# Cross-attention over 32 batches: context rows loaded as 120 and 5 partitions, a slot earlier, with all statistics of a batch in one VectorE slot

## The chip, the cores and the metric

One Trainium2 chip, one core. The metric is the device time of one execution in microseconds (us); the kernel before has three runs, and one profiled execution from which every row below is taken.

## The reference

Inputs are x (32 batches x 112 tokens x 512), a context (32 x 375 x 512), a mask (32 x 375, all true), four 512 x 512 weights, gamma, beta and a gate. All is float32.

```
a   = layer_norm(context) * gamma + beta          # over the 512 features of each of the 375 rows
Q   = x @ Wq.T ;  K = a @ Wk.T ;  V = a @ Wv.T     # split into 16 heads of 32
p   = softmax(mask(Q @ K.T / sqrt(32)))            # 112 x 375 for each batch and head
out = x + tanh(gate) * ((p @ V) @ Wo.T)
```

## The kernel before

**Layout.** The context comes in twice: transposed (`ctxT`, features on partitions) into `cn`, which is what K and V are computed from, and by rows (`ctx`) into `rows`, which serves the layer norm's statistics alone. `rows` holds one batch as 125 partitions of 3 context rows each (3 x 512 floats, 6 KB on a partition, 750 KB in all); there is one such buffer. VectorE computes `bn_stats` on the three chunks and `bn_aggr` on the results, GpSimd makes -mean and 1/std of them (`row_statistics`), SyncE stores these in DRAM (`row_stats`), and a broadcast load brings them back to all 128 partitions (`stat_bc`, 375 KB). GpSimd then centres, scales and applies gamma and beta to `cn`.

**Products.** K, V, Q and the output projection are each computed as three float32r products (high and low parts). A batch is four slots, u = 0 to 3, of four heads each; the loop body is LOOP = 8 slots, two batches. In slot r TensorE does the K projection of item r + 1, a V projection of one 125-row chunk (in slots u = 3, 0, 1) or the output projection (u = 2), the scores of item r and the weighted sum of item r - 3.

**The exchange of maxima.** The softmax maximum of each slot is found by going through DRAM. In slot r VectorE reduces the scores of item r - 1 (`quadrant_maxima`, L708), SyncE stores the result (L318, `row_max`, 21 KB) and, when that has landed, loads it back spread out (L323, `x4`, which the profile names x, 84 KB). VectorE in slot r + 1 reduces the loaded tile (L695), spreads it (L698) and subtracts it from the scores (L718); ScalarE exponentiates (L584). SyncE's part is strictly serial:

```python
sync.wait_ge(quad_max, i * LOOP + r)
if behind(i, LOOP, r - 1):
    wait_apart(sync, ld_max, i * (16 * LOOP) + (r - 1) * 16)
sync.dma_start(row_max.rearrange("t (q k) -> q t k", q=HC), rmax[:, :]).then_inc(max_stored, 16)
wait_apart(sync, max_stored, i * (16 * LOOP) + r * 16)
...
sync.dma_start(x4[:, :], bass.AP(...)).then_inc(ld_max, 16)
```

So there is one store and one load a slot, and the next store waits for the last load. The order within each engine's slot is written by hand:

- VectorE: `quadrant_maxima` of item r - 1, `row_maximum` and `subtract_maximum` of item r - 2, at u = 3 `normalise`, at u = 0 the low part of the attention output, at u = 1 the statistics' first chunk, at u = 2 the other two chunks and `bn_join`, and then at u = 2 `result` (L689), which empties the PSUM bank of the output projection. TensorE's V projection in the slot after (u = 3) waits for that (`y_done`), because it writes the same bank.
- ScalarE: `scores_out` of item r - 1 (L553), the exponentials of item r - 3 (L584), `weighted_out` (L569); at u = 3 the three loads on its own DMA queue, in the order statistics (L259), transposed context (L247), rows (L253); then the copy of K out of PSUM (L606), the high part of the context (L521) and the copy of V (L613).
- The rows load of batch c + 5 waits for `stats_done` of batch c + 4, as there is one `rows` buffer. `stats_done` is what `bn_join` signals.

Ahead of the slots is a prologue: weights and x come in, Q is computed for all batches, and the rows of batches 0 to 3 are loaded from SyncE's queue (L253 as well) and their statistics computed.

Of the kernel before, what the change touches and what calls it, by code (L numbers as in the profile page):

```python
# [12 lines left out]
B, T, S, D = 32, 112, 375, 512  # L13
# [3 lines left out]
ST, SP_ = 3, 125  # L17
# [16 lines left out]
def xattn(nc, xT, x, ctx, ctxT, mask, wqT, wkT, wvT, woT, gamma, beta, gate, out, row_stats):  # L34
    es = ExitStack()
    with es:
        def sb(name, shape, dt=F32):
            return es.enter_context(nc.sbuf_tensor(name, shape, dt))

        def sem(name):  # L40
            return es.enter_context(nc.semaphore(name))
# [64 lines left out]
        rows = sb("rows", [128, ST, D])  # L106
# [32 lines left out]
        ld_rows = sem("ld_rows")  # L139
# [27 lines left out]
        stats_done = sem("stats_done")  # L167
        ln_step = sem("ln_step")
        row_stat_done = sem("row_stat_done")
# [35 lines left out]
        rows_v = ctx.rearrange("b (p j) d -> b p j d", j=ST)  # L205
# [5 lines left out]
        def live(i, k, shift, count):  # L211
            return not isinstance(i, int) or 0 <= k * i + shift < count

        def behind(i, k, shift):
            return not isinstance(i, int) or k * i + shift > 0

        def first_two(i, c):
            return isinstance(i, int) and 2 * i + c < 2

        def wait_apart(engine, s, value):  # L220
            engine.wait_ge(s, value)
            if not isinstance(value, int):
                engine.sem_inc(passed)
# [19 lines left out]
        def is_slot(i, r, n):  # L243
            return isinstance(i, int) and LOOP * i + r == n

        def load_ctx(queue, i, c):
            queue.dma_start(cn[:, c % 2, :, :], ctxT_v[i * 2 + c, :, :, :]) \  # L247
                .then_inc(ld_ctx[c % 2], 16)

        def load_rows(queue, i, c):  # L250
            if behind(i, 2, c):
                wait_apart(queue, stats_done, i * 2 + c)
            queue.dma_start(rows[0:SP_, :, :], rows_v[i * 2 + c, :, :, :]).then_inc(ld_rows, 16)  # L253

        def load_stats(queue, i, c):
            wait_apart(queue, stat_stored, i * 32 + (c + 1) * 16)
            if behind(i, 2, c):
                wait_apart(queue, divided, i * LOOP + c * KT)
            queue.dma_start(stat_bc[:, :, :].rearrange("p w s -> p (w s)"),  # L259
                           row_stats[bass.ds(i * 2 + c, 1), :].partition_broadcast(128)  # L260
                           .rearrange("p a s -> p (a s)")).then_inc(ld_stat, 16)
# [229 lines left out]
        def _(act):  # L491
# [52 lines left out]
            def scores_out(i, r):  # L544

                c, u = divmod(r - 1, KT)
                act.wait_ge(s_mm, i * LOOP + r)
                if u == 0:
                    act.wait_ge(bias_done, i * 2 + (c + 1))
                if isinstance(i, int) and LOOP * i + r - 1 < NB:  # L550
                    act.wait_ge(low_done, r)
                for j in range(ST):
                    act.activation(prob[0:SP_, (r - 1) % NB, j, :].rearrange("p (h t) -> p h t", h=HC),  # L553
                                   sbank[0:SP_, :, T * j:T * j + T], ACT.Identity,
                                   bias=mask_b[0:SP_, c % 2, j:j + 1]).then_inc(s_out, 1)
# [16 lines left out]
            def slot(i, r):  # L572
                c, u = divmod(r, KT)
                if is_slot(i, r, 0):
                    act.wait_ge(mask_mm, 1)
                    act.activation(maskT[0:SP_, :, :],
                                   bank[PB][0:SP_, 0:ST * B].rearrange("p (j b) -> p j b", j=ST),
                                   ACT.Copy).then_inc(mask_out, 1)
                if live(i, LOOP, r - 1, SLOTS):
                    scores_out(i, r)  # L580
                if live(i, LOOP, r - 3, SLOTS):
                    for j in range(ST):
                        act.wait_ge(sub_done, i * (LOOP * ST) + ((r - 3) * ST + j + 1))
                        act.activation(prob[0:SP_, (r - 3) % NB, j, :], prob[0:SP_, (r - 3) % NB, j, :],  # L584
                                       ACT.Exp, scale=SCALE).then_inc(exp_done, 1)
                if live(i, LOOP, r - 4, SLOTS):
                    weighted_out(i, r)
                if u == 3:
                    if live(i, 2, c + 3, B) and behind(i, 2, c + 1):
                        load_stats(act, i, c + 3)  # L590
                    if live(i, 2, c + 3, B) and not first_two(i, c + 3):
                        wait_apart(act, c_done, i * LOOP + (c + 2) * KT)
                        load_ctx(act, i, c + 3)
                    if live(i, 2, c + 5, B) and behind(i, 2, c + 2):
                        load_rows(act, i, c + 5)
                if u == 0 and live(i, 2, c - 2, B):
                    b = c - 2
                    act.wait_ge(o_norm, i * 2 + (b + 1))
                    if behind(i, 2, b):
                        act.wait_ge(y_mm, i * 2 + b)  # L600
                    act.activation(oT[:, 0, :, :].rearrange("p c t -> p (c t)"),
                                   pv[:, b % 2 * HT:b % 2 * HT + HT], ACT.Copy).then_inc(o_hi, 1)

                if live(i, LOOP, r + 1, SLOTS):
                    act.wait_ge(k_mm, i * LOOP + (r + 2))
                    act.activation(kT[:, (r + 1) % 2, :], bank[KB][:, 0:SE], ACT.Copy) \  # L606
                        .then_inc(k_done, 1)
                if not early(i, r):
                    context_hi(i, r)
                vc, j = v_item(r)  # L610
                if j is not None and live(i, 2, vc, B):
                    act.wait_ge(v_mm, i * (2 * ST) + (vc * ST + j + 1))
                    act.activation(v_sb[0:SP_, vc % 2, j, :], bank[VO[r % 2]][0:SP_, :], ACT.Copy) \  # L613
                        .then_inc(v_done, 1)

            slots(act, slot)

        @block.vector
        def _(dve):
# [20 lines left out]
                split(xraw[:, g, :, :], xr[:, g, 0, :, :], xr[:, g, 1, :, :],  # L640
                      xr_hi, i * 2 + g, xr_done)

            def bn_rows(i, c, chunks):
                if chunks[0] == 0:
                    dve.wait_ge(ld_rows, i * 32 + (c + 1) * 16)
                    if not first_two(i, c):
                        dve.wait_ge(row_stat_done, i * 2 + (c - 1))
                    if isinstance(i, int) and 2 * i + c > 0:
                        dve.wait_ge(stats_done, 2 * i + c)
                for j in chunks:  # L650
                    dve.bn_stats(stats[0:SP_, j, :], rows[0:SP_, j, :]).then_inc(bn_step, 1)  # L651

            def bn_join(i, c):
                wait_apart(dve, bn_step, i * (2 * ST) + (c + 1) * ST)
                for j in range(ST):
                    last = dve.bn_aggr(mv[0:SP_, c % 2, j, :], stats[0:SP_, j, :])  # L656
                last.then_inc(stats_done, 1)

            def statistics(i, c):
                bn_rows(i, c, range(ST))  # L660
                bn_join(i, c)

            def weight_lo(n, raw, dst):
                for k in range(KT):
# [70 lines left out]
            def slot(i, r):  # L735
                c, u = divmod(r, KT)
                if live(i, LOOP, r - 1, SLOTS):
                    quadrant_maxima(i, r)
                if live(i, LOOP, r - 2, SLOTS):
                    row_maximum(i, r)  # L740
                    subtract_maximum(i, r)
                if u == 3 and live(i, 2, c - 1, B):
                    normalise(i, c - 1)
                if u == 0 and live(i, 2, c - 2, B):
                    b = c - 2
                    dve.wait_ge(o_hi, i * 2 + (b + 1))
                    dve.tensor_tensor(oT[:, 1, :, :].rearrange("p c t -> p (c t)"),  # L747
                                      pv[:, b % 2 * HT:b % 2 * HT + HT],
                                      oT[:, 0, :, :].rearrange("p c t -> p (c t)").bitcast(F32),
                                      ALU.subtract).then_inc(o_done, 1)  # L750
                if u == 1 and live(i, 2, c + 4, B) and behind(i, 2, c + 2):
                    bn_rows(i, c + 4, (0,))
                if u == 2 and live(i, 2, c + 4, B) and behind(i, 2, c + 2):
                    bn_rows(i, c + 4, (1, 2))
                    bn_join(i, c + 4)
                if u == 2 and live(i, 2, c - 2, B):
                    result(i, c - 2)

# [187 lines left out]
```

## Time and profile before

| | |
|---|---|
| runs (us) | 1159.52, 1155.87, 1161.36; median 1159.52 |
| profiled execution's own time | 1151.25 us |
| span in the profile | 1149.4 us |
| mean granted TensorE clock | 0.953 |
| busy | PE 89%, PEld 74%, DVE 67%, POOL 59%, ACT 56% |
| DMA | 102.26 MB, 89 GB/s mean; ScalarE's queue (q10) 56.60 MB, SyncE's (q1) 44.94 MB |

PE is TensorE, PEld its weight loads, DVE VectorE, ACT ScalarE, POOL GpSimd, SP SyncE; SPq and ACTq are the issuing queues of those engines. In a wait row the engine and its line stand left of the arrow, and what it waited for right of it. A clock of 1.00 is 2.4 GHz, 0.50 is 1.2 GHz. Most runs agree closely, and a difference of under 0.5% can't be told from none.

### The profile page before, as it was taken

What the parts mean: (1) busy time and instruction counts of PE and PEld (TensorE: products, weight loads), DVE (VectorE), ACT (ScalarE), POOL (GpSimd) and SP (SyncE); (2) the same over time, 40 slices, a digit from 0 to 9 for tenths busy, and PEclk for the clock granted to TensorE, in tenths of its full rate; (3) what the DMA queues carried; (4) which work ended last, traced back from release to release, by engine and by line L of the source; (5) the groups of instructions that cost most, each with busy time, mean ns of one, the idle gap of its engine ahead of it and who ended that gap; (6) DMA issues with size and microseconds to landing.
All of it is one profiled execution on the core that took longest, in us unless ns stands there. A gap on an engine that the chain in (4) does not pass through costs nothing.

```text
span 1149.4 us, 31949 instructions
## 1 busy us (share of the span) xinstructions
PE 1025.9 (89%) x11665; PEld 852.0 (74%) x11665; DVE 774.2 (67%) x1446; ACT 645.2 (56%) x1332; POOL 680.7 (59%) x945
## 2 busy tenths in 40 slices
PE   8796989989989989899898889898889898999995
PEld 7795877778777767687777767777777677878873
DVE  4640477776676677667666777666767866787775
ACT  2312565665565656565556656655556566666662
POOL 1346866666666756567557556676566556776211
PEclk9898999999999999999999999999999999999997
DMA  9443222222232332223323322232233222322111
GB/s 274 158 148 71 98 78 75 88 72 86 86 97 87 97 95 82 66 75 89 95 86 97 94 80 78 66 96 87 87 96 95 84 78 68 94 76 73 33 33 40
DMA packets 82772, 102.26 MB, mean 89 GB/s; under 512 B 28544, under 2 KB 65408, under 8 KB 82720
## 3 DMA queue, kind: packets, MB, share of 16 engines
q10 hardware_dynamic: 24232, 56.60, 15.1%
q1 hardware_dynamic: 58488, 44.94, 14.5%
q8 instruction: 35, 0.57, 0.2%
q14 instruction: 17, 0.14, 0.0%
HBM read 91.34 MB, written 10.19 MB: 88 GB/s over the span
## 4 chain that ended last, share of the span: by engine, by line
DMA 65%; DVE 16%; PE 12%; issue 4%; POOL 2%; SPq 1%; ACT 0%; DVEq 0%; ACTq 0%; POOLq 0%
DMA row_max<-rmax 34%; DMA x<-row_max 25%; PE bank L765 9%; DVE rmax L708 4%; DVE shared_f L718 3%; DVE stats L651 3%; DMA rows<-in_ctx 3%; DMA row_stats<-row_stat 3%; DVE bank L698 2%; PE sbank L859 1%; DVE top L695 1%; PE bank L875 1%; DVE mv L656 1%; DMA shared_f<-in_xT 1%; POOL cn L408 0%
## 5 line engine op out<-in xcount | busy, mean ns | idle before, releaser
L765 PE MATMUL bank<-w_v,shared_r 128*125 128x512 f32 x1152 | 312.5, 424 | 77.0 <-DVE xy L689 77.0
L765 PEld LDWEIGHTS bank<-w_v,shared_r 128*125 128x125 f32 x1152 | 229.6, 202 | 135.9 <-issue 84.2
L708 DVE TRANSPOSE_TENSOR_REDUCE rmax<-shared_f 128x14 f32<-128x448 f32 x384 | 216.3, 614 | 158.5 <-DMA row_max<-rmax 131.1
L765 PE MATMUL bank<-shared_r,w_k 128*128 128x376 f32 x1536 | 300.7, 345 | 10.1 <-ACT shared_f L606 9.5
L765 PEld LDWEIGHTS bank<-shared_r,w_k 128*128 128x128 f32 x1536 | 260.8, 190 | 32.2 <-issue 20.9
L584 ACT ACTIVATE shared_f<-shared_f 125x448 f32<-125x448 f32 x384 | 204.3, 580 | 133.9 <-DVE shared_f L718 133.8
L438 POOL TENSOR_TENSOR shared_f<-shared_f 125x448 f32<-125x448 f32 x128 | 151.0, 1179 | 177.9 <-ACT shared_f L584 164.7
L553 ACT ACTIVATE shared_f<-sbank,mask_b 125x448 f32<-125x448 f32 x384 | 215.6, 635 | 69.2 <-PE sbank L859 69.1
L718 DVE TENSOR_TENSOR shared_f<-shared_f,bank 125x448 f32<-125x448 f32 x384 | 215.5, 617 | 4.5
L613 ACT ACTIVATE shared_f<-bank 125x512 f32<-125x512 f32 x96 | 57.3, 597 | 160.2 <-PE bank L765 160.1
L695 DVE TENSOR_REDUCE top<-x 128x14 f32<-128x168 f32 x128 | 56.0, 437 | 120.9 <-DMA x<-row_max 120.9
L859 PEld LDWEIGHTS sbank<-shared_f 32*125 32x125 f32 x3072 | 96.3, 185 | 49.6 <-issue 49.2
L428 POOL TENSOR_TENSOR shared_r<-cn,shared_r 128x375 fp32r<-128x375 f32 x128 | 117.7, 920 | 21.5 <-ACT shared_r L521 20.4
L408 POOL TENSOR_TENSOR cn<-cn,stat_bc 128x375 f32<-128x375 f32 x128 | 116.4, 943 | 20.6 <-DMA stat_bc<-row_stats 16.8
L392 POOL TENSOR_SCALAR row_stat<-mv 125x3 f32<-125x3 f32 x32 | 8.0, 251 | 202.4 <-DVE mv L656 202.4
L859 PE MATMUL sbank<-shared_f 32*125 32x112 f32 x3072 | 119.0, 284 | 0.8 <-ACT shared_f L553 0.8
L414 POOL TENSOR_TENSOR cn<-cn,stat_bc 128x375 f32<-128x375 f32 x128 | 118.7, 962 | 0.2
L875 PE MATMUL bank<-shared_f 125*32 125x112 f32 x3072 | 101.2, 265 | 12.5 <-ACT shared_f L569 12.3
L765 PE MATMUL bank<-w_o,shared_r 128*112 128x512 f32 x384 | 97.1, 402 | 4.0 <-DVE shared_r L747 4.0
L606 ACT ACTIVATE shared_f<-bank 128x376 f32<-128x376 f32 x128 | 61.9, 483 | 56.3 <-DVE mv L656 49.8
L875 PEld LDWEIGHTS bank<-shared_f 125*32 125x32 f32 x3072 | 70.0, 110 | 27.9 <-ACT shared_f L569 15.3
L698 DVE STREAM_TRANSPOSE bank<-top 128x448 f32<-128x448 f32 x128 | 84.5, 660 | 4.4
(64 smaller groups left out, 950.6 us busy)
## 6 DMA issues: line engine op xcount, KB each, us to landing
cn<-in_ctxT ACTq DMA_DIRECT2D x30, 750.0 KB, 6.2
rows<-in_ctx ACTq DMA_DIRECT2D x28, 750.0 KB
stat_bc<-row_stats ACTq DMA_DIRECT2D x29, 375.0 KB, 4.2
x<-row_max SPq DMA_DIRECT2D x128, 84.0 KB
xy<-in_x SPq DMA_DIRECT2D x32, 224.0 KB, 3.1
out<-xy SPq DMA_DIRECT2D x32, 224.0 KB, 4.9
shared_f<-in_xT SPq DMA_DIRECT2D x7, 896.0 KB, 8.4
rows<-in_ctx SPq DMA_DIRECT2D x4, 750.0 KB
```

What stands on the lines that cost most here:

```text
L408: pool.tensor_tensor(cn[:, c % 2, k, :], cn[:, c % 2, k, :], stat_bc[:, 0, :], ALU.add).then_inc(centred, 1)
L414: pool.tensor_tensor(cn[:, c % 2, k, :], cn[:, c % 2, k, :], stat_bc[:, 1, :], ALU.mult).then_inc(divided, 1)
L428: pool.tensor_tensor(cT[:, p, 1, k, 0:S], cn[:, p, k, :], cT[:, p, 0, k, 0:S].bitcast(F32), ALU.subtract) \
L438: pool.tensor_tensor(psum[0:SP_, :], prob[0:SP_, q, 0, :], prob[0:SP_, q, 1, :], ALU.add).then_inc(sum_done, 1)
L553: act.activation(prob[0:SP_, (r - 1) % NB, j, :].rearrange("p (h t) -> p h t", h=HC), sbank[0:SP_, :, T * j:T * j + T], ACT.Identity, bias ...
L584: act.activation(prob[0:SP_, (r - 3) % NB, j, :], prob[0:SP_, (r - 3) % NB, j, :], ACT.Exp, scale=SCALE).then_inc(exp_done, 1)
L698: dve.transpose(spread.rearrange("p (k a) -> p k a", a=32), top[:, :].unsqueeze(2).to_broadcast([128, BLK, 32])) \
L708: last = dve.tensor_reduce(rmax[:, BLK * j:BLK * j + BLK], prob[:, (r - 1) % NB, j, :].rearrange("p (k a) -> p k a", a=32), AX.X, ALU.max, ...
L718: dve.tensor_tensor(prob[0:SP_, (r - 2) % NB, j, :], prob[0:SP_, (r - 2) % NB, j, :], spread[0:SP_, :], ALU.subtract).then_inc(sub_done, 1)
L765: last = pe.matmul(dst, l, m, start=(start and k == 0), stop=(stop and k == len(pairs) - 1))
L859: last = pe.matmul(bank[h][0:SP_, T * j:T * j + T], kT[part, r % 2, SP_ * j:SP_ * j + SP_], qs[part, c % 2, u, :], start=True, stop=True)
L875: pe.matmul(bank[PB][HD * h:HD * h + HD, 0:T], v_sb[0:SP_, c % 2, j, col:col + HD], prob[0:SP_, (r - 3) % NB, j, T * h:T * h + T], start=( ...
```

## The change

`load_rows` issues two transfers in place of one: partitions 0 to 119 and partitions 120 to 124, both on the same semaphore, so that a batch now counts 32 in place of 16. On ScalarE the rows load moves from slot u = 3, where it stood behind the statistics and context loads, to slot u = 2, directly after `weighted_out`. On VectorE `bn_rows` and `bn_join` become one function; all three `bn_stats` and the three `bn_aggr` now run in slot u = 1, and slot u = 2 has no statistics any more. The bytes moved and the arithmetic are the same. `load_rows` serves the prologue's four loads too.

```
@@ load_rows @@
             if behind(i, 2, c):
                 wait_apart(queue, stats_done, i * 2 + c)
-            queue.dma_start(rows[0:SP_, :, :], rows_v[i * 2 + c, :, :, :]).then_inc(ld_rows, 16)
+            for part in (slice(0, 120), slice(120, SP_)):
+                queue.dma_start(rows[part, :, :], rows_v[i * 2 + c, part, :, :]).then_inc(ld_rows, 16)
@@ ScalarE, slot @@
                         load_ctx(act, i, c + 3)
-                    if live(i, 2, c + 5, B) and behind(i, 2, c + 2):
-                        load_rows(act, i, c + 5)
+                if u == 2 and live(i, 2, c + 5, B) and behind(i, 2, c + 2):
+                    load_rows(act, i, c + 5)
@@ VectorE @@
-            def bn_rows(i, c, chunks):
-                if chunks[0] == 0:
-                    dve.wait_ge(ld_rows, i * 32 + (c + 1) * 16)
...
-            def bn_join(i, c):
+            def statistics(i, c):
+                dve.wait_ge(ld_rows, i * 64 + (c + 1) * 32)
+                if not first_two(i, c):
+                    dve.wait_ge(row_stat_done, i * 2 + (c - 1))
+                if isinstance(i, int) and 2 * i + c > 0:
+                    dve.wait_ge(stats_done, 2 * i + c)
+                for j in range(ST):
                     dve.bn_stats(stats[0:SP_, j, :], rows[0:SP_, j, :]).then_inc(bn_step, 1)
                 wait_apart(dve, bn_step, i * (2 * ST) + (c + 1) * ST)
                 for j in range(ST):
                     last = dve.bn_aggr(mv[0:SP_, c % 2, j, :], stats[0:SP_, j, :])
                 last.then_inc(stats_done, 1)
...
@@ VectorE, slot @@
                 if u == 1 and live(i, 2, c + 4, B) and behind(i, 2, c + 2):
-                    bn_rows(i, c + 4, (0,))
-                if u == 2 and live(i, 2, c + 4, B) and behind(i, 2, c + 2):
-                    bn_rows(i, c + 4, (1, 2))
-                    bn_join(i, c + 4)
+                    statistics(i, c + 4)
```

## Rows read from the trace of the kernel before

**Rows 1.** The page: busy time of the engines, chain that ended last.

```profile
PE 1025.9 (89%) x11665; PEld 852.0 (74%) x11665; DVE 774.2 (67%) x1446; ACT 645.2 (56%) x1332; POOL 680.7 (59%) x945
...
DMA 65%; DVE 16%; PE 12%; issue 4%; POOL 2%; SPq 1%; ACT 0%; DVEq 0%; ACTq 0%; POOLq 0%
```

**Rows 2.** Waits in 259.6 to 946.5 us: total, times, longest (us).

```profile
DVE rmax L708 <- DMA row_max<-rmax: 102.2, 21, 5.4
...
PE bank L765 <- DVE xy L689: 65.9, 21, 4.3
```

**Rows 3.** Stretches: length; PE, PEld, DVE, ACT, POOL busy; clock; DMA share; GB/s.

```profile
259.60:946.50 686.90, 618.19 (x7397) 507.97 (x7396) 482.42 (x925) 406.08 (x840) 435.04 (x610) 0.96 0.29 86
...
1041.00:1111.00 70.00, 70.00 (x891) 58.54 (x884) 52.05 (x93) 46.35 (x99) 28.47 (x32) 1.00 0.14 38
```

**Rows 4.** Timeline of SyncE's queue: start, duration, instruction.

```profile
514.58 0.54 SPq L318 DMA_DIRECT2D row_max<-rmax  x1
516.87 0.54 SPq L323 DMA_DIRECT2D x<-row_max  x1
521.47 0.53 SPq L318 DMA_DIRECT2D row_max<-rmax  x1
531.11 0.53 SPq L323 DMA_DIRECT2D x<-row_max  x1
534.50 0.53 SPq L318 DMA_DIRECT2D row_max<-rmax  x1
...
540.59 0.56 SPq L318 DMA_DIRECT2D row_max<-rmax  x1
...
547.47 0.54 SPq L318 DMA_DIRECT2D row_max<-rmax  x1
```

**Rows 5.** Timeline of ScalarE and its queue, slots u = 2 and 3.

```profile
511.63 0.47 ACT L606 ACTIVATE shared_f<-bank 128x376 f32<-128x376 f32 x1
...
518.44 0.39 ACTq L247 DMA_DIRECT2D cn<-in_ctxT  x1
519.27 0.29 ACTq L253 DMA_DIRECT2D rows<-in_ctx  x1
```

**Rows 6.** Timeline of TensorE: K projection, then V projection, of slot u = 3.

```profile
515.19 2.32 PE L765 MATMUL bank<-shared_r,w_k 128*128 128x376 f32 x12
519.91 4.59 PE L765 MATMUL bank<-w_v,shared_r 128*125 128x512 f32 x12 [2.39 <-DVE xy L689]
```

**Rows 7.** Timeline of VectorE: statistics at the end of slots u = 1 and 2.

```profile
510.79 0.69 DVE L651 BATCH_NORM_STATS2 stats<-rows 125x6 f32<-125x512 f32 x1
...
517.30 1.28 DVE L651 BATCH_NORM_STATS2 stats<-rows 125x6 f32<-125x512 f32 x2
...
519.01 0.75 DVE L689 SCALAR_TENSOR_TENSOR xy<-bank,gat,xy 112x512 f32<-112x512 f32 x1
```

**Rows 8.** Busy time by stretch, columns as in rows 3.

```profile
525.00:527.00 2.00, 2.00 (x59) 1.72 (x53) 1.25 (x2) 1.71 (x5) 2.00 (x4) 1.00 0.33 137
...
1010.00:1012.00 2.00, 2.00 (x27) 1.45 (x29) 1.93 (x4) 0.51 (x1) 1.67 (x4) 1.00 0.90 324
```

**Rows 9.** ScalarE's queue at the last context load, which no rows load follows.

```profile
1034.90 0.45 ACTq L247 DMA_DIRECT2D cn<-in_ctxT  x1
```

**Rows 10.** SyncE's queue: first u = 3 store, the last two, and the load after.

```profile
135.66 0.53 SPq L318 DMA_DIRECT2D row_max<-rmax  x1
...
1009.92 0.53 SPq L318 DMA_DIRECT2D row_max<-rmax  x1
...
1035.83 0.53 SPq L318 DMA_DIRECT2D row_max<-rmax  x1
1041.09 0.53 SPq L323 DMA_DIRECT2D x<-row_max  x1
```

**Rows 11.** Waits in 95 to 120 us, where the slots begin.

```profile
PE bank L765 <- ACT shared_f L606: 9.5, 1, 9.5
```

**Rows 12.** The page: packets, MB and share of ScalarE's DMA queue.

```profile
q10 hardware_dynamic: 24232, 56.60, 15.1%
```

More of the change, by code:

```diff
@@ L641, in x_group @@
                       xr_hi, i * 2 + g, xr_done)
-            def bn_rows(i, c, chunks):
-                if chunks[0] == 0:
-                    dve.wait_ge(ld_rows, i * 32 + (c + 1) * 16)
[L646 to L650, printed above, removed]
+            def statistics(i, c):
[5 more added lines that the diff above has]
+                for j in range(ST):
                     dve.bn_stats(stats[0:SP_, j, :], rows[0:SP_, j, :]).then_inc(bn_step, 1)
-            def bn_join(i, c):
                 wait_apart(dve, bn_step, i * (2 * ST) + (c + 1) * ST)
@@ L657, in bn_join @@
                 last.then_inc(stats_done, 1)
-            def statistics(i, c):
-                bn_rows(i, c, range(ST))
-                bn_join(i, c)
             def weight_lo(n, raw, dst):
```

## The prediction

> **What bounds the kernel now.** I read four views in this order. The page first: TensorE is busy 89% of the span, yet the chain that ended last is 65% DMA and 12% PE [rows 1]. So there are two candidates for the bound, and they must be held against each other in the steady part. The waits of the loop say how they meet: TensorE's only large wait is the V projection on VectorE's `result` (`y_done`), 65.9 us in 21 batches, 3.1 each, and VectorE's largest is on the store of the maxima, 102.2 us, 4.9 each [rows 2]. The stretches give both lengths. The store of slot u = 3 comes first at 135.66 and last with a rows load at 1009.92, 27 batches later: 874.3 / 27 = 32.38 us a batch [rows 10]. From 1041 to 1111, where no rows or context load is left, TensorE is busy all 70 of 70 us at clock 1.00 and does ten slots, 28.0 us a batch [rows 3]. So TensorE's floor is 28.0, and 4.4 us a batch are someone else's.
>
> SyncE's queue shows whose. Name by L0, L1 the landing of the exchange's load in slots u = 0 and 1; the next store is issued there. The four intervals between stores of one batch are 6.9 (u = 2 to 3), 13.0 (u = 3 to 0), 6.1 and 6.9 [rows 4]. The 13.0 is a store that takes 9.64 where its neighbour takes 2.29, and a load of 3.39. The context load was issued 3.0 us ahead of it, and the rows load 2.2 ahead [rows 4, 5]. The store ends at 531.1, 11.8 us after the rows load was issued, and the rows load is what it waits out: from 525 to 527 the DMA engines are busy 0.33 of 16, about five engines, moving 137 GB/s, while a context load of the same 750 KB, with nothing behind it, keeps them at 0.90 and 324 GB/s [rows 8]. At the last context load, which no rows load follows, the store waits only until 6.2 us after the context's issue [rows 9, 10]. TensorE then pays twice: it waits 2.39 for `result`, and its V projection takes 4.59 us [rows 6]; mean clock in the loop is 0.96 against 1.00 later [rows 3].
>
> **The change part by part.**
>
> *The split.* Before, the load runs on about 5 of 16 engines for its whole length. The new 120-partition piece has no row before. From below: 750 KB at the 324 GB/s of rows 8 is 2.4 us, plus the 2.3 that a bare store takes from issue to landing [rows 4], 4.7. From above: the 6.2 of the context load, which had the 375 KB of statistics ahead of it. The two-issue form adds one 0.29 us issue [rows 5]. I take 5.2 + 0.3 = 5.5, nearest to the like-sized context load less the statistics' share (375 KB / 324 = 1.2). Range 4.7 to 6.5. On ScalarE 28 more issues of 0.29 are 8 us, on an engine that is 56% busy: nothing on the path, unless it is what TensorE waits for.
>
> The Trainium skill ("DMA: Bandwidth & Descriptors", section on why a DMA increments its semaphore by 16) says that a transfer uses the largest number up to 16 that divides the slowest dimension: 5 for 125 partitions, 15 for 120, 5 for 5, and 4 for the exchange, whose DRAM side leads with 4. The trace agrees: ScalarE's queue has 24232 packets [rows 12], and its 30 context loads at 512 + 16 and its 33 statistics and x loads at 128 + 16 leave 3640, which is 28 x (125 + 5). By this rule the busiest engine carries 54 KB in place of 150, at 137 / 5 = 27 GB/s some 2.0 us, and the load lands 4.3 us after its issue, just under my lower bound; the sum below would not change, since the context load then ends last.
>
> *The statistics on VectorE.* Slot u = 2 loses the stretch from 517.30 to 519.01, 1.7 us [rows 7], ahead of `result`: `y_done` comes 1.7 us sooner after the subtraction. Slot u = 1 gains it: 0.7 becomes 2.4. There, after L0: reduce, spread and subtract end at 517.30 - 514.58 = 2.7, statistics 2.4, maxima of the next slot 1.7 (from 519.76 to the store at 521.47): L0 + 6.8. The interval from L0 to L1 is 6.9, so the store at L1 is not late, by 0.1; if the u = 0 interval's store got faster, it would be late by up to 1. I book 0.1.
>
> *The moved rows load.* ScalarE now waits in slot u = 2 for `stats_done` at L0 + 5.1. Before, it started the K copy at 511.63 [rows 5], 0.8 us after the statistics began; now the two issues are done 2.4 + 0.6 = 3.0 after that begin, so the K copy, the high part and the next slot's `scores_out` stand 2.2 us later. Cover: the next K projection starts at 515.19 [rows 6], 3.1 us after the K copy's end before: 0.9 is left. If this cover were gone it would cost up to 2.2 a batch. At u = 3 ScalarE loses its wait on the statistics.
> The DMA side: issued at L0 + 5.4 = L1 - 1.5, landed at L1 + 4.0. The store of slot u = 2, issued at L1 + 0.1, would land at L1 + 2.4 and now lands with it: 1.6 late. Load 3.4: the slot u = 3 store is issued at L1 + 7.5. The context load goes out 1.1 us after the subtraction (518.44 against 517.30), L1 + 3.9, and lands 6.2 later, L1 + 10.1; the store would have landed at L1 + 9.8, so 0.3 late; with its load the exchange is at L1 + 13.5. Adding 6.1 and 6.9: 26.5 us. If rows and context load delay each other in full (6.5 for rows, context later by the 2.4 of its data), it is 28.9. GpSimd's `row_statistics` no longer waits, since its input is there a slot earlier.
>
> *Sum.* The exchange needs 26.5 to 28.9, TensorE 28.0. With two loops of nearly one length the slower sets the pace and neither gets its slack back at once: I take 28.3. 27 x (32.38 - 28.3) = 110 us. The batches behind 1009.92 have no rows load and stay.
> *Prologue.* The slots' start waits 9.5 us [rows 11] for a ScalarE that stands behind the statistics of batch 3, whose rows were under way beside a context load. Landing some 6 us sooner, as in 11.8 against 5.5, gives 6 (3 to 9.5).
> Against its own time: 1151.25 - 110 - 6 = 1035. The runs' median is 8.3 above that time; part of it should be the disturbed exchange itself, so I carry half: 1039.
>
> **The rivals.**
> 1. *The split does not spread the load.* The move alone then works. Rows at 137 GB/s take 750 / 137 = 5.5, plus 2.3: 7.8 from issue, landing L1 + 6.3; the store of u = 2 is 3.9 late, the next is issued at L1 + 9.8, context is landed by then or soon after, and two slots take 15.5: 28.5 to 29.5 a batch, 27 x 3.4 + 3 = 95 saved, 1060. For it: nothing in the trace shows a 120-partition load. Against it: the 0.33 beside the 0.90 [rows 8]. The Trainium skill (same page, "Rules for kernel authors") says not to bother with two transfers on disjoint partition halves, as they share the engines and serialise; for this load of 125 partitions, whose one form fills a third of the engines, rows 8 speak against applying it.
> 2. *DMA still ends last.* The u = 3 store meets the context load at its worst, as at 1035.83 where it took 5.26 [rows 10], 3.0 over a bare one, the u = 2 store is 2.4 late, and the K copy's 2.2 comes through half: 5.8 + 2.4 + 5.7 + 3.0 + 13.0 + 1.1 = 31.0; saved 27 x 1.4 + 6 = 44, 1111. For it: exchange is 65% DMA now. Against: the two delays come one after the other, and cover each other.
> 3. *Slower: two collisions in place of one.* Rows and context loads met the exchange in one slot before; now each meets its own store. If the rows load at u = 2 costs the 7.35 it costs at u = 3, and the context load its 3.0, a batch is 24.5 + 10.4 = 34.9, 27 x 2.5 = 68 more, on the median 1227. It decides once the two delays together pass 32.4 - 24.5 = 7.9. Against it: my terms are 1.6 and 0.3, and in rival 1 3.9.
>
> **How the numbers follow.** Forecast 0.68, own range 1026 (28.0 a batch and 9.5 in the prologue give 1024, with nothing of the 8.3) to 1055. Rival 1 0.15, rival 2 0.11, rival 3 0.04, and 0.02 for no difference. With 0.2 left outside: 1024 to 1085, which holds the forecast and most of rival 1. A measurement here tells no change from 0.5%. Faster 0.94, same 0.02, slower 0.04.
>
> **What would show it.** In the trace after: the u = 3 store under 4 us, the u = 2 store 3 to 5; u = 3 stores 28 to 29 us apart; no stretch at 0.33 DMA; the V projection's wait on `result` near nothing and its twelve matmuls under 3.2 us; TensorE busy 97% and a chain of PE rather than DMA; the wait at the slots' start 3 to 4 us. Wrong would make it: a rows load that still takes 8 us, a VectorE or ScalarE wait that grows into TensorE's, or a clock that does not hold 1.00 over some 800 us of unbroken work, of which the trace shows 70.

## The result and the profile after

The changed kernel takes 1086.15 us (median; 1083.24 to 1088.33, 4 runs) against 1157.69 for the kernel before: a ratio of 0.938, 95% interval 0.934 to 0.942. Run again on another chip it gave 0.940 (0.936 to 0.944). The change makes the kernel 6% faster. I had predicted 1039 with a range of 1024 to 1085: the direction was right, the saving I expected was 1.7 times the measured one (120.5 against 71.5 us), and the time lies just outside the range.

The page of the changed kernel, with the busy times, ScalarE's DMA queue and the chain that ended last:

```profile
PE 1000.0 (92%) x11665; PEld 831.0 (77%) x11665; DVE 783.0 (72%) x1446; ACT 651.6 (60%) x1332; POOL 690.4 (64%) x945
...
q10 hardware_dynamic: 24652, 56.60, 20.3%
...
DMA 51%; DVE 25%; PE 14%; issue 6%; POOL 2%; SPq 1%; ACT 1%; DVEq 1%; ACTq 0%; POOLq 0%
```

Against [rows 1] DMA fell from 65% of the chain to 51%, but it still leads; I had expected TensorE to lead. The same queue has 420 more packets than in [rows 12], 15 for each of its 28 rows loads.

The stretches and the waits of the changed kernel's loop, with the columns of [rows 3] and [rows 2]:

```profile
265.06:876.50 611.44, 569.08 (x7068) 468.36 (x7064) 465.78 (x881) 392.11 (x802) 422.94 (x580) 1.00 0.36 92
```

```profile
POOL cn L409 <- DMA cn<-in_ctxT: 59.0, 20, 3.4
DVE rmax L702 <- DMA row_max<-rmax: 36.5, 20, 2.3
PE bank L756 <- ACT shared_f L607: 21.7, 24, 1.9
PE bank L756 <- DVE xy L683: 16.3, 20, 1.4
```

This stretch is 20 batches long: 30.57 us each, TensorE busy 28.45 of them, 93%. TensorE's wait for `result` fell from 3.1 to 0.8 us a batch, and the clock is at 1.00 where it was 0.96. A new wait has come up, 1.1 us a batch: the K projection waits for ScalarE's K copy. So TensorE is close to its floor of 28.0, yet something still sets 30.6.

SyncE's queue in one batch of the changed kernel, from the load of slot u = 1 to the store of the next batch's u = 2, and the first u = 3 store and the one 27 batches later:

```profile
125.81 0.53 SPq L319 DMA_DIRECT2D row_max<-rmax  x1
...
292.44 0.54 SPq L324 DMA_DIRECT2D x<-row_max  x1
296.10 0.56 SPq L319 DMA_DIRECT2D row_max<-rmax  x1
301.65 0.54 SPq L324 DMA_DIRECT2D x<-row_max  x1
306.85 0.53 SPq L319 DMA_DIRECT2D row_max<-rmax  x1
309.14 0.54 SPq L324 DMA_DIRECT2D x<-row_max  x1
313.56 0.53 SPq L319 DMA_DIRECT2D row_max<-rmax  x1
...
319.49 0.56 SPq L319 DMA_DIRECT2D row_max<-rmax  x1
...
326.29 0.54 SPq L319 DMA_DIRECT2D row_max<-rmax  x1
...
942.62 0.53 SPq L319 DMA_DIRECT2D row_max<-rmax  x1
```

ScalarE's queue in the same batch:

```profile
294.48 0.79 ACTq L254 DMA_DIRECT2D rows<-in_ctx  x2
295.46 0.48 ACT L607 ACTIVATE shared_f<-bank 128x376 f32<-128x376 f32 x1 [2.61 <-issue]
...
300.01 0.41 ACTq L247 DMA_DIRECT2D cn<-in_ctxT  x1
```

Two transfers of the exchange are long. The u = 2 store takes 5.55 us; the rows load was issued 1.6 us ahead of it. The load that follows takes 5.20; the context load was issued 1.6 us ahead of that. That these two loads are the cause is shown by tiny_rows and tiny_ctx below. In [rows 4] it was one, the u = 3 store with 9.64. The long slot is now 10.75 us in place of 13.0.

The packets of the DMA queues show how the small transfer waits (q1 is SyncE's queue, q10 ScalarE's; packets, MB, share of 16 engines). The four windows are 296.1 to 299.9, from the store's issue on, in which only ScalarE's queue moves anything; 299.9 to 300.4; 301.65 to 304.6, from the load's issue on, again with ScalarE's queue alone; and 304.6 to 306.4:

```profile
q10 hardware_dynamic: 131, 0.71, 70.0%
...
q1 hardware_dynamic: 132, 0.02, 24.4%
q10 hardware_dynamic: 5, 0.00, 4.8%
...
q10 hardware_dynamic: 444, 0.74, 91.8%
...
q10 hardware_dynamic: 162, 0.22, 32.9%
q1 hardware_dynamic: 132, 0.09, 14.8%
```

So it is the data that waits and not only the message that it has landed: none of the store's 132 packets moves until the rows load is nearly through, 3.8 us after the store's issue. On the mean of 21 batches they begin 3.3 us after it, and 1.2 us in tiny_rows, where the rows load moves next to nothing.

The table below gives the mean of each piece over 21 batches, from SyncE's queue (store: issue of store to issue of load; load: from there to the next store's issue, with what VectorE does meanwhile; us).

| kernel | u = 2 store, load | u = 3 store, load | u = 0 slot | u = 1 slot | batch | ratio to before |
|---|---|---|---|---|---|---|
| before | 2.29, 4.56 | 9.73, 3.32 | 6.19 | 6.64 | 32.72 | 1 |
| changed | 5.25, 5.45 | 2.28, 4.51 | 6.20 | 6.90 | 30.54 | 0.938 |
| split_only | 2.29, 4.56 | 7.81, 3.24 | 6.18 | 6.57 | 30.64 | 0.950 |
| move_only | 7.80, 4.34 | 2.28, 4.51 | 6.29 | 6.87 | 32.11 | 0.988 |
| stats_one_slot | 2.29, 3.55 | 10.53, 3.27 | 6.23 | 6.84 | 32.82 | 1.005 |
| late_issue | 5.31, 5.39 | 2.28, 4.51 | 6.05 | 6.89 | 30.39 | 0.947 |
| change_again | 5.24, 5.48 | 2.28, 4.51 | 6.08 | 6.96 | 30.52 | 0.940 |
| no_tail | 4.82, 5.86 | 2.28, 4.52 | 6.10 | 6.88 | 30.44 | 0.939 |
| tiny_rows | 2.29, 3.71 | 5.70, 3.24 | 6.18 | 6.91 | 27.97 | 0.881 |
| tiny_ctx | 5.26, 3.37 | 2.28, 4.51 | 6.29 | 6.88 | 28.60 | 0.893 |
| sp_issue | 2.29, 4.70 | 2.84, 4.20 | 7.93 | 11.35 | 33.33 | 1.005 |
| rows_sp | 2.30, 3.58 | 7.56, 3.23 | 6.44 | 6.96 | 29.92 | 0.924 |
| rows_sp_whole | 2.30, 3.87 | 10.55, 3.30 | 6.38 | 6.91 | 33.30 | 1.013 |
| sp_pool_order | 2.30, 3.54 | 4.11, 3.71 | 8.57 | 6.95 | 29.12 | 0.902 |

### The profile page after: what moved, and what is told of

It is laid out like the page before. It is cut to its first block, busy times and chain, and to the rows that moved or that the text cites. A ratio compares the mean times of both kernels' runs of the same rounds, so it can differ in the third digit from the quotient of the medians.

```text
span 1083.2 us, 32025 instructions
## 1 busy us (share of the span) xinstructions
PE 1000.0 (92%) x11665; PEld 831.0 (77%) x11665; DVE 783.0 (72%) x1446; ACT 651.6 (60%) x1332; POOL 690.4 (64%) x945
## 4 chain that ended last, share of the span: by engine, by line
DMA 51%; DVE 25%; PE 14%; issue 6%; POOL 2%; SPq 1%; ACT 1%; DVEq 1%; ACTq 0%; POOLq 0%
DMA x<-row_max 26%; DMA row_max<-rmax 21%; PE bank L756 8%; DVE shared_f L712 6%; DVE rmax L702 6%; DVE stats L651 3%; DVE bank L692 3%; DVE top L689 2%; PE bank L772 2%; DVE bank L722 2%; DVE dsum L717 1%; PE sbank L850 1%; DMA row_stats<-row_stat 1%; DMA shared_f<-in_xT 1%; PE bank L866 1%
## 5 line engine op out<-in xcount | busy, mean ns | idle before, releaser
L756 PE MATMUL bank<-w_v,shared_r 128*125 128x512 f32 x1152 | 286.4, 397 | 22.0 <-DVE xy L683 22.0
L585 ACT ACTIVATE shared_f<-shared_f 125x448 f32<-125x448 f32 x384 | 206.5, 581 | 126.1 <-DVE shared_f L712 125.7
L756 PEld LDWEIGHTS bank<-w_v,shared_r 128*125 128x125 f32 x1152 | 211.3, 186 | 74.4 <-issue 29.1
L409 POOL TENSOR_TENSOR cn<-cn,stat_bc 128x375 f32<-128x375 f32 x128 | 116.1, 940 | 105.7 <-DMA cn<-in_ctxT 91.7
L415 POOL TENSOR_TENSOR cn<-cn,stat_bc 128x375 f32<-128x375 f32 x128 | 130.5, 1053 | 0.2
L756 PEld LDWEIGHTS bank<-w_o,shared_r 128*112 128x112 f32 x384 | 68.6, 180 | 24.0 <-DVE shared_r L741 4.3
```

Source lines behind the costliest of these rows:

```text
L409: pool.tensor_tensor(cn[:, c % 2, k, :], cn[:, c % 2, k, :], stat_bc[:, 0, :], ALU.add).then_inc(centred, 1)
L415: pool.tensor_tensor(cn[:, c % 2, k, :], cn[:, c % 2, k, :], stat_bc[:, 1, :], ALU.mult).then_inc(divided, 1)
L756: last = pe.matmul(dst, l, m, start=(start and k == 0), stop=(stop and k == len(pairs) - 1))
```

## The experiments

The kernels fall in three groups, each run on its own chip; the kernel before had medians of 1147.03, 1153.40 and 1154.66 there, so the ratios are compared, not the times. Across chips even the ratios agree only to about one hundredth: late_issue, which differs from the changed kernel by 0.15 us a batch, has 0.947 on the first chip, where the changed kernel was not run, and the changed kernel has 0.938 and 0.940 on others. Differences smaller than that are read from runs of one chip, or from the batches of the table.

### The parts of the change by themselves

**split_only**: `load_rows` of the changed kernel and its count of 32, everything else as before.

```
-            queue.dma_start(rows[0:SP_, :, :], rows_v[i * 2 + c, :, :, :]).then_inc(ld_rows, 16)
+            for part in (slice(0, 120), slice(120, SP_)):
+                queue.dma_start(rows[part, :, :], rows_v[i * 2 + c, part, :, :]).then_inc(ld_rows, 16)
```

> The kernel before with the rows load cut into 120 and 5 partitions and nothing else: the load stays in slot u = 3 behind statistics and context, and the statistics stay spread over slots u = 1 and 2. Theory A (what the exchange pays is the time until the bulk loads issued ahead of it have drained, so their total length counts and not the slot): the u = 3 store falls from 9.6 us to 5 to 6, the batch from 32.7 to 28.5 to 29.5 us, and the time to 1055 to 1080, no worse than the changed kernel. Theory B (the move is what gained most): 1120 to 1145.

Measured: 1085.93 us, ratio 0.950 (0.946 to 0.953). SyncE's queue of split_only around its u = 3 slot:

```profile
301.60 0.53 SPq L319 DMA_DIRECT2D row_max<-rmax  x1
310.13 0.54 SPq L324 DMA_DIRECT2D x<-row_max  x1
313.52 0.53 SPq L319 DMA_DIRECT2D row_max<-rmax  x1
```

The split alone has nearly the whole gain: 30.64 us a batch against 30.54 of the changed kernel, and 0.950 against late_issue's 0.947 on the same chip. This speaks for theory A, but the store fell to 7.8 us on the mean (8.5 in the rows shown) and the batch to 30.6, not to the 5 to 6 and 28.5 to 29.5 that I had expected: three loads in a row, statistics, context and rows, are still all ahead of it. The time is outside the range I gave theory A by 6 us.

**move_only**: the changed kernel with `load_rows` as one transfer of 125 partitions.

```
-            for part in (slice(0, 120), slice(120, SP_)):
-                queue.dma_start(rows[part, :, :], rows_v[i * 2 + c, part, :, :]).then_inc(ld_rows, 16)
+            queue.dma_start(rows[0:SP_, :, :], rows_v[i * 2 + c, :, :, :]).then_inc(ld_rows, 16)
```

> The changed kernel with the rows load as one transfer of 125 partitions again; load and statistics keep their new slots. Theory A: the load runs on about five engines for 6 us and more, the u = 2 store waits for its end, 7 to 8 us where the changed kernel has 5.3, and the time is 1095 to 1120. Theory B: within 10 us of the changed kernel's 1086.

Measured: 1133.27 us, ratio 0.988 (0.983 to 0.993). SyncE's queue of move_only at one u = 2 slot:

```profile
313.88 0.54 SPq L318 DMA_DIRECT2D row_max<-rmax  x1
323.10 0.54 SPq L323 DMA_DIRECT2D x<-row_max  x1
326.74 0.53 SPq L318 DMA_DIRECT2D row_max<-rmax  x1
```

The u = 2 store takes 9.2 here and 7.8 on the mean, in place of 5.25. Theory B is out. The time is 13 us above even theory A's range. Move and statistics without the split gain 0.6 us a batch (32.11 against 32.72).

**stats_one_slot**: the kernel before with `statistics(i, c + 4)` at u = 1 and nothing at u = 2; the load as before.

```
                 if u == 1 and live(i, 2, c + 4, B) and behind(i, 2, c + 2):
-                    bn_rows(i, c + 4, (0,))
-                if u == 2 and live(i, 2, c + 4, B) and behind(i, 2, c + 2):
-                    bn_rows(i, c + 4, (1, 2))
-                    bn_join(i, c + 4)
+                    statistics(i, c + 4)
```

> The kernel before with only the VectorE part of the change: all statistics in slot u = 1, the rows load undivided in slot u = 3. Theory A: the u = 3 store is issued up to 1 us sooner and lands at the same point of the rows load, so nothing moves: 1150 to 1160. Rival (result behind the statistics was the bound, 1.7 us a batch): 1110 to 1120.

Measured: 1154.12 us, ratio 1.005 (1.002 to 1.008). The u = 2 load became 1.0 us shorter and the u = 3 store 0.8 longer, as theory A has it: the store is issued sooner and ends at the same point. VectorE's part gains nothing by itself.

**late_issue**: the changed kernel with the rows load behind the K copy and the high part.

```
-                if u == 2 and live(i, 2, c + 5, B) and behind(i, 2, c + 2):
-                    load_rows(act, i, c + 5)
...
                 if not early(i, r):
                     context_hi(i, r)
+                if u == 2 and live(i, 2, c + 5, B) and behind(i, 2, c + 2):
+                    load_rows(act, i, c + 5)
```

> The changed kernel with the rows load in slot u = 2 moved behind the K copy and the high part of the context on ScalarE, so that these no longer stand behind its wait for the statistics. Rival (the ScalarE stall costs TensorE the 1.1 us a batch that its K projection waits for the K copy): 1055 to 1065. Theory A: the load is issued about 1 us later and its end, which the u = 2 store waits for, is up to 1 us later too: 1086 to 1110, not faster.

Measured: 1082.83 us, ratio 0.947 (0.943 to 0.950). The load was not issued later at all, since `stats_done` comes at the same time anyway; ScalarE's queue of late_issue:

```profile
292.53 0.47 ACT L605 ACTIVATE shared_f<-bank 128x376 f32<-128x376 f32 x1
...
294.34 0.78 ACTq L254 DMA_DIRECT2D rows<-in_ctx  x2
```

The K copy of slot u = 2 runs at 292.5 and no longer behind the wait (295.46 above), and the batch is 30.39 us against 30.52 to 30.54. The time is 3 us below theory A's range, whose later issue did not come about, and far above the rival's. The wait of ScalarE in u = 2 thus costs 0.15 us a batch at most. TensorE's wait for the K copy stayed (17.8 us in 19 batches), so it is another one: it is ScalarE's copy in slot u = 0. There the copy stands behind the high part of the attention output, which waits 1.2 us a batch for VectorE's `normalise`, and that began late because the maxima came late.

### What the bytes cost

**change_again** is the changed kernel, as the yardstick of this group.

> The changed kernel itself, on this chip beside the others: a ratio of 0.93 to 0.95 against the kernel before, as it had. It is the yardstick for the other three.

Measured: 1085.11 us, ratio 0.940 (0.936 to 0.944).

**no_tail**: the last five partitions of the in-slot rows load cut to 16 bytes each.

```
+            tail = slice(120, SP_)
...
+                queue.dma_start(rows[tail, 0, 0:4], rows_v[i * 2 + c, tail, 0, 0:4]).then_inc(ld_rows, 16)
```

> The changed kernel with the 5-partition piece of the in-slot rows load reduced to 16 bytes on each partition (batches 4 to 31 keep old rows in those five partitions; same count of transfers). If the tail, which lies on engines that the first piece also uses, ends the load: 0.5 to 1 us a batch, 12 to 25 us less than the changed kernel. If the shared memory rate ends it: within 5 us of it.

Measured: 1084.45 us, ratio 0.939 (0.935 to 0.943), no difference. The store is 0.4 us shorter and the next load 0.4 longer, for that one ends with the context load. The tail costs nothing.

**tiny_rows**: both pieces of the in-slot rows load cut to 16 bytes.

```
+                for part in (slice(0, 120), slice(120, SP_)):
+                    queue.dma_start(rows[part, 0, 0:4], rows_v[i * 2 + c, part, 0, 0:4]).then_inc(ld_rows, 16)
```

> The changed kernel with both pieces of the in-slot rows load reduced to 16 bytes on each partition (the statistics of batches 4 to 31 are then of old rows; same count of transfers, same waits). It shows what the 750 KB still cost. Theory A: the u = 2 store falls from 5.3 to about 2.3 to 3 us, a batch is 28.0 to 28.5, 1015 to 1035. Rival (the order on ScalarE and VectorE costs it): 1060 or more.

Measured: 1016.21 us, ratio 0.881 (0.878 to 0.884). The u = 2 store is 2.29 us, as theory A has it, and a batch is 27.97 us: TensorE's floor. The page of tiny_rows:

```profile
PE 987.4 (97%) x11665; PEld 829.6 (82%) x11665; DVE 792.8 (78%) x1446; ACT 635.9 (63%) x1332; POOL 691.7 (68%) x945
...
PE 84%; DMA 8%; DVE 4%; POOL 2%; issue 1%; SPq 1%; ACT 1%; ACTq 0%; DVEq 0%; POOLq 0%
```

So all that the changed kernel has over 28.0, 2.55 us a batch, goes when the 750 KB of rows go, and none of it is set by the new order of ScalarE or VectorE alone, which this run has too. The context load now meets the u = 3 store alone, 5.70 in place of 2.28, and that can be borne.

**tiny_ctx**: the same for the in-slot context load, rows whole.

```
+                queue.dma_start(cn[:, c % 2, 0, 0:4], ctxT_v[i * 2 + c, :, 0, 0:4]) \
+                    .then_inc(ld_ctx[c % 2], 16)
```

> The changed kernel with the in-slot context load reduced to 16 bytes on each partition (batches 3 to 31 are then computed from old context; same count of transfers, same waits). It shows what the 750 KB of context cost the exchange. Theory A: the u = 2 load, issued 1.6 us behind the context, falls from 5.45 to 3.6 to 4.2 us and GpSimd's wait for the context goes; a batch 28.3 to 29.2, ratio 0.89 to 0.91. By the prediction's term of 0.3 us a batch: 0.93 or more.

Measured: 1028.96 us, ratio 0.893 (0.889 to 0.897). The u = 2 load fell from 5.45 to 3.37, and the other pieces moved by 0.2 at most. The context costs the exchange 2.1 us a batch, where my sum had 0.3. The savings of tiny_rows and tiny_ctx (2.55 and 1.9 us a batch) do not add up: the kernel has only 2.55 over TensorE's floor, and without the rows the context load meets another transfer. The u = 2 store is as long as before (5.26 against 5.25), although the whole context load is issued 1.6 us before that store ends: a transfer already under way is not held up by it.

### Where the loads are issued

**sp_issue**: the changed kernel with all three loads taken from ScalarE and put into SyncE's slot, each behind the exchange's own load.

```
                 if live(i, LOOP, r - 1, SLOTS):
                     exchange_maxima(i, r)
+                if u == 2 and live(i, 2, c + 5, B) and behind(i, 2, c + 2):
+                    load_rows(sync, i, c + 5)
+                if u == 3:
...
+                        load_stats(sync, i, c + 3)
...
+                        load_ctx(sync, i, c + 3)
```

> The changed kernel with rows, statistics and context loads issued by SyncE, rows in slot u = 2 and the others in u = 3, each directly behind the exchange's own load of that slot, in place of ScalarE. Theory A: each bulk load then has the exchange's load of 3.5 us to drain beside it, and only what is left after that delays the next store: 1 to 2 us for rows, 2 to 3 for context, a batch of 28.5 to 29.5, 1040 to 1065. Rival (the place of issue does not matter, only the bytes): within 10 us of the changed kernel.

Measured: 1159.26 us, ratio 1.005 (1.002 to 1.007), and both expectations fell. SyncE's queue of sp_issue at u = 2 and 3, and the waits of its loop:

```profile
313.33 0.54 SPq L319 DMA_DIRECT2D row_max<-rmax  x1
315.62 0.53 SPq L324 DMA_DIRECT2D x<-row_max  x1
316.49 0.82 SPq L254 DMA_DIRECT2D rows<-in_ctx  x2
320.32 0.56 SPq L319 DMA_DIRECT2D row_max<-rmax  x1
323.17 0.53 SPq L324 DMA_DIRECT2D x<-row_max  x1
```

```profile
POOL cn L417 <- DMA cn<-in_ctxT: 143.2, 18, 8.7
...
PE bank L875 <- POOL shared_f L447: 54.7, 18, 3.8
```

The exchange did what theory A says, and better: the rows load, issued 0.9 us behind the exchange's load, made the next store only 0.55 us longer (2.84 on the mean), and the context load made the one behind it 1.7 longer. But GpSimd now waits 8 us a batch for the context, and its `sum_chunks` stands behind the centring that needs it; TensorE waits 3.0 us a batch for that sum. A collision was traded for a late transfer.

**rows_sp**: only the rows load goes to SyncE.

```
-                if u == 2 and live(i, 2, c + 5, B) and behind(i, 2, c + 2):
-                    load_rows(act, i, c + 5)
...
                     exchange_maxima(i, r)
+                if u == 2 and live(i, 2, c + 5, B) and behind(i, 2, c + 2):
+                    load_rows(sync, i, c + 5)
```

> The changed kernel with only the rows load (two pieces) issued by SyncE in slot u = 2, directly behind the exchange's own load; statistics and context stay with ScalarE at u = 3. Theory A (an exchange transfer waits for the bulk issued ahead of it, not for the bulk behind it): the u = 2 store falls from 5.2 to 2.3 us and the u = 2 load from 5.45 to under 5, while the u = 3 store now waits for the context load, 5 to 7 us; a batch is 29 to 30 us where the changed kernel has 30.5, ratio 0.90 to 0.93. Rival (the same bytes on the same engines cost the same, wherever they are issued): ratio 0.935 to 0.945, as the changed kernel.

Measured: 1066.03 us, ratio 0.924 (0.921 to 0.926). The same bytes in the same slot, issued behind the exchange's load and not ahead of its store: store 2.30, load 3.58, and the u = 3 store takes 7.56, a little over the expected 5 to 7. Theory A holds, the rival is out. This run changes the queue as well as the moment of issue. The changed kernel itself tells them apart: there ScalarE issues the same rows from its own queue 2.0 us behind the exchange's load of slot u = 1 (294.48 against 292.44), and that slot takes 6.90 to 6.96 us, against 6.91 in tiny_rows. So a bulk load behind a small one costs it nothing from the other queue either.

**rows_sp_whole**: as rows_sp, with one transfer of 125 partitions (the edit of move_only).

> As rows_sp, but with the rows load as one transfer of 125 partitions. Theory A: its 7 us of draining reach past the exchange's load of 3.5 and into the u = 3 store and the context load behind it; a batch is 1 to 2 us longer than in rows_sp, ratio 0.94 to 0.97. Rival (behind the exchange's load the length is hidden): within 0.01 of rows_sp.

Measured: 1169.64 us, ratio 1.013 (1.009 to 1.016). The u = 3 store takes 10.55, a batch is 3.4 us longer than in rows_sp. The ratio is above the range I gave theory A: the split is worth 9 hundredths here.

**sp_pool_order**: sp_issue with GpSimd's sum ahead of its centring.

```
+                if live(i, LOOP, r - 3, SLOTS):
+                    sum_chunks(i, r)
                 if live(i, 2, c + 2, B) and not first_two(i, c + 2):
                     if u == 0:
                         center(i, c + 2, (0, 1, 2, 3))
...
-                if live(i, LOOP, r - 3, SLOTS):
-                    sum_chunks(i, r)
```

> The run in which SyncE issues rows, statistics and context, which gave 1.005, with one more edit: GpSimd computes the slot's sum_chunks before it centres, divides or scales the context. If that run was slow because the sum stood behind a centring that waited for a late context load (TensorE waited 54.7 us for it in 18 batches, 3.0 a batch), this gives 0.92 to 0.95. If the late context is the cost in itself (ScalarE's high part needs it), it stays at 0.98 or more.

Measured: 1040.54 us, ratio 0.902 (0.899 to 0.904), better than I had expected and the best of the runs that compute the whole reference: against the changed kernel's 0.938 to 0.940, on other chips, it is 4% faster again. The stretch 265 to 865 of sp_pool_order, and its page:

```profile
265.00:865.00 600.00, 582.10 (x7226) 481.45 (x7225) 473.66 (x902) 393.49 (x826) 422.86 (x592) 1.00 0.36 96
```

```profile
PE 995.1 (95%) x11665; PEld 830.5 (80%) x11665; DVE 777.0 (75%) x1446; ACT 639.4 (61%) x1332; POOL 677.5 (65%) x945
```

TensorE is busy 97% of the loop. sp_issue was slow because of the order on GpSimd and not because of where its loads were issued.

## Why the prediction was wrong

**The bound** was read rightly: the exchange, disturbed by the rows load, held TensorE back through `result`, and TensorE's floor is 28.0. tiny_rows reached 27.97.

**The sum.** By the profiled executions the change saved 1151.25 - 1084.97 = 66.3 us. The 27 batches from the first u = 3 store (125.81) to the one at 942.62 take 30.25 us each against 32.38: 57.5 saved, where I had 110. The slots begin 9.9 sooner (135.66 - 125.81), where I had 6 and a range of 3 to 9.5: the wait at their start fell by 3.6 us (9.5 to 5.9), and VectorE's wait for the rows ahead of it by another 4.4, which I had not counted. The rest gave back 1.1. So the step that failed is the length of the exchange, "26.5", and with it the "28.3" a batch. From the u = 2 store's issue, L1 + 0.1, to L1 + 13.5 I had 13.4 us for the slots u = 2 and 3; they take 10.70 + 6.79 = 17.5. The 4.1 between are three terms:

- *"1.6 late"*, the rows load against the u = 2 store: 2.96 measured (5.25 - 2.29), 1.4 more. By the landings in the trace, on the mean of 21 batches, the rows load lands 6.25 us after its issue where I had 5.5. That is 0.75 of the 1.4, and inside my 4.7 to 6.5. The store lands another 0.4 behind it, where I had both land at once, and SyncE takes 0.2 from there to the next issue. I had taken the length from the context load's 6.2 less the statistics at its best rate, 324 GB/s [rows 8]; rows in two pieces move at 240 (last section), which for 750 KB is some 0.8 us longer. A load of x of 224 KB, issued 1.1 us ahead by SyncE, was left out; no run shows what it costs.
- *"Load 3.4"*, with the context load's delay booked at 0.3 on the next store: 5.45 measured against 3.5 from L1 + 4.0 to L1 + 7.5, 2.0 more. The context was issued where I had said, at L1 + 4.0, and landed 6.4 later, about where I had said. But I took the exchange's load, issued 1.6 us behind it, to pass it. It did not: it ended at 306.8, L1 + 10.8, 0.4 after the context. tiny_ctx measures the term directly, 2.1. This is the main fault, for I had seen the same thing in the store of [rows 4] and had not applied it to the load.
- *The u = 3 slot at 6.0*, from L1 + 7.5 to L1 + 13.5 (a store of 2.3 with 0.3, and a load of 3.4): 6.79. I had left out `normalise`, which VectorE does in that slot. The changed kernel's VectorE timeline:

```profile
306.80 0.45 DVE L689 TENSOR_REDUCE top<-x 128x14 f32<-128x168 f32 x1 [3.50 <-DMA x<-row_max]
...
309.58 0.64 DVE L717 TRANSPOSE_TENSOR_REDUCE dsum<-shared_f 128x14 f32<-128x448 f32 x1
...
311.76 1.69 DVE L702 TRANSPOSE_TENSOR_REDUCE rmax<-shared_f 128x14 f32<-128x448 f32 x3
```

From the landing at 306.8 to the end of the maxima at 313.45 are 6.7 us, 2.2 of them `normalise` (309.58 to 311.76), and the store goes out at 313.56: VectorE sets this slot, not the transfers. In the kernel before, this work was done while the long store of the same slot was under way. No run takes `normalise` out, so its 0.8 is read from the timeline alone.

**The mechanism** of each part: the split is what gains (split_only 0.950, move_only 0.988). On top of the split, the move and the order on VectorE add 0.1 us a batch (30.64 to 30.54): one collision of 5.5 us in the u = 3 store (7.81 - 2.29) became two, of 3.0 and 2.1. VectorE's part gains nothing alone (1.005): `result` came 1.7 us sooner, but the exchange held the batch. The cover for ScalarE's wait was enough, as I had said (late_issue, 0.15 us a batch). Of the signs I had named, the u = 3 store under 4 (2.28), the twelve matmuls of the V projection under 3.2 (3.03 at 299.71) and a clock of 1.00 came; u = 3 stores 28 to 29 us apart, TensorE busy 97% (93% in the loop) and a chain of PE did not.

**The rivals.** Rival 1, that the split does not spread the load, is out: move_only's store is 2.5 us longer, and a batch of move_only is 32.1 us, where I had put such a kernel at 28.5 to 29.5. That price had the same fault in it. Rival 2, that DMA still ends last, is what happened, at 30.5 us a batch where I had 31.0; I gave it 0.11. Its time, 1111, was 25 us too long. Its mechanism was half right: the u = 2 store is 3.0 late where it had 2.4, but the other 2.1 came on the load behind it and not on the u = 3 store, and the 1.1 it had for the K copy is 0.15 at most (late_issue). Against it I had argued that "the two delays come one after the other, and cover each other". They come one after the other and add up, for each has a transfer of the exchange of its own to delay, and the exchange has but one in flight. Rival 3 had this, two collisions in place of one, with prices too high: 3.0 + 2.1 = 5.1 against its threshold of 7.9. move_only comes near it, at 5.5 on its store.

The Trainium skill's rule on how many engines a transfer uses ("DMA: Bandwidth & Descriptors", section on why a DMA increments its semaphore by 16) gives 15 and 5 engines for the two pieces and 5 for the one. With one packet for each partition and one more for each engine that is 145 packets (120 + 15 and 5 + 5) against 130. The trace agrees: there are 15 more for each load. The 4.3 us to landing that I had worked out with it was too short; 6.25 were measured. The Trainium skill's advice not to bother with two transfers on disjoint partition halves (same page, "Rules for kernel authors") gives as its reason that both halves use all 16 engines. The trace does not bear it out for a load of 125 partitions, whose one form keeps 0.33 of them busy: the split is worth 4 to 5% here (1133.27 us of move_only against 1083 to 1088 of the changed kernel; 32.11 against 30.54 a batch) and 9% in rows_sp.

## What to carry to other kernels

When a chain of small dependent transfers shares the DMA engines with bulk loads, as here, ask of each bulk load which small transfer is issued next behind it. In this kernel that one paid until the bulk had drained, and the one already under way paid nothing. So shorten the bulk (a partition count that spreads), and issue it right behind a small transfer rather than ahead of one. Then check who consumes the load, and put urgent work of that engine ahead of the wait for it. And when a long piece leaves a slot, list all work of every engine in that slot again, for what it covered is the next bound.

## What the runs showed of the hardware

- A transfer of 125 partitions kept the DMA engines at 0.33 and 137 GB/s [rows 8]. Cut into 120 and 5, the loop's two microseconds 297 to 299 of the changed kernel, with rows under way, show 0.94 and 240 GB/s. A context load shows 0.90 and 324 [rows 8], so a like busy share need not mean a like rate:

```profile
297.00:299.00 2.00, 1.52 (x9) 1.21 (x8) 1.97 (x5) 2.00 (x5) 1.62 (x4) 1.00 0.94 240
```

- A store of 21 KB issued from SyncE 1.6 us behind a 750 KB load of ScalarE's queue took 5.25 us on the mean in place of 2.29, and its first packet moved 3.3 us after its issue in place of 1.2: the data itself waited, across two queues. A load of 84 KB issued 0.9 us ahead of the same 750 KB took 3.58 (rows_sp), against 3.37 with no context load ahead of it (tiny_ctx) and 3.39 in [rows 4]. In this kernel the order of issue decided, over both queues. What in the DMA hardware makes it so was not measured.
- The TensorE clock held 1.00 over the 600 us of sp_pool_order's loop at 97% busy.
